# Moving the second pair's normalisation and the weight transposes within the first feed-forward stage of a gated multi-layer kernel

## What is computed

```python
def act_quant(x):                      # per token
    scale = 128.0 / clip(max(abs(x)), 1e-5)
    return clip(round(x * scale), -128, 127) / scale

gate = act_quant(x) @ ternary(w_gate).T        # 256 -> 1024
up   = act_quant(x) @ ternary(w_up).T
h    = silu(gate) * up
y    = act_quant(fwht(h)) @ ternary(w_down).T  # 1024 -> 256, fwht: Walsh-Hadamard transform
x    = x + tanh(g_ffn[1]) * y
```

## Time and profile before

| | |
|---|---|
| median of 3 runs | 758.43 us (758.4 to 760.88) |
| the profiled execution | 758.4 us, its span 756.6 us |
| PE busy | 673.2 us (89%), 4446 matmuls |
| DVE busy | 537.9 us (71%) |
| ACT busy | 350.4 us (46%) |
| POOL busy | 217.3 us (29%) |

### The profile page before, as it was taken

How to read it: one execution, slowest core, us unless ns; L and a number is a source line. 1 busy time by engine, 2 the same in 40 slices (tenths; PEclk the granted TensorE clock), 3 DMA queues, 4 the chain that set the end, 5 groups by cost and what they waited for, 6 DMA issues and landing times. The chain is left out here.

```text
span 756.6 us, 13927 instructions
## 1 busy us (share of the span) xinstructions
PE 673.2 (89%) x4446; PEld 461.8 (61%) x4446; DVE 537.9 (71%) x1622; ACT 350.4 (46%) x620; POOL 217.3 (29%) x308
## 2 busy tenths in 40 slices
PE   8999979798987987899779999986788999999997
PEld 4644566775864665587667787553243327777776
DVE  5687988877988788878866563747986957425545
ACT  2673545565464765142116325335488794122220
POOL 1001596101100033111314552632343220523330
PEclk9999996998999999989999999997799999999999
DMA  6997521050000050000063160012000043233214
GB/s 182 342 248 136 166 85 55 4 169 0 3 3 1 9 161 1 1 0 1 29 197 111 52 216 22 29 37 78 2 3 2 3 154 78 71 102 109 93 56 173
DMA packets 55565, 60.23 MB, mean 80 GB/s; under 512 B 13847, under 2 KB 48808, under 8 KB 55496
## 3 DMA queue, kind: packets, MB, share of 16 engines
q1 hardware_dynamic: 50408, 46.02, 21.4%
q0 software_dynamic: 4848, 13.28, 5.0%
q10 hardware_dynamic: 240, 0.05, 0.0%
HBM read 34.92 MB, written 24.20 MB: 78 GB/s over the span
## 5 line engine op out<-in xcount | busy, mean ns | idle before, releaser
L2040 ACT ACTIVATE arenas<-psum 128x512 f32<-128x512 f32 (+6 forms) x89 | 63.1, 732 | 52.6 <-PE psum L1188 46.2
L3342 DVE TENSOR_REDUCE arenas<-psum 128x2 f32<-128x512 f32 x96 | 61.8, 684 | 12.6 <-PE psum L1791 11.2
L996 POOL TENSOR_SCALAR arenas<-arenas,small 128x1024 f32<-128x1024 f32 x8 | 9.0, 1127 | 147.6 <-DVE small L3029 147.6
L1188 PE MATMUL psum<-conb,shared 128*128 128x128 bf16 (+2 forms) x512 | 39.2, 234 | 12.1 <-POOL shared L1001 5.1
L1013 POOL DMA_INDIRECT experts_l<-shared,small x30 | 29.7, 991 | 65.2 <-ACT shared L2348 54.9
L1188 PEld LDWEIGHTS psum<-conb,shared 128*128 128x128 bf16 (+2 forms) x512 | 34.7, 121 | 20.4 <-issue 12.8
L2040 ACT ACTIVATE late<-psum 128x512 f32<-128x512 f32 (+1 forms) x51 | 25.7, 504 | 40.8 <-PE psum L1188 40.8
L1188 PE MATMUL psum<-con,early 128*128 128x128 f32 (+1 forms) x188 | 32.5, 283 | 10.7 <-DVE early L2721 2.9
L2395 ACT ACTIVATE early<-psum 128x1024 f32<-128x1024 f32 x32 | 32.0, 1031 | 17.6 <-PE psum L1808 17.3
L1675 PE MATMUL psum<-early,late 128*128 128x256 f32 x128 | 33.4, 411 | 5.3 <-DVE early L3235 5.2
L1675 PE MATMUL psum<-arenas,early 128*128 128x256 f32 x160 | 36.7, 383 | 0.7 <-DVE arenas L3496 0.7
(11 more groups left out here) (455 smaller groups left out, 1780.4 us busy)
## 6 DMA issues: line engine op xcount, KB each, us to landing
sorted_l<-late SPq DMA_DIRECT2D x3, 1920.0 KB, 18.0
early<-sorted_l SPq DMA_DIRECT2D x6, 645.0 KB, 5.8
early<-in_L_ffn_sw SPq DMA_DIRECT2D x3, 1024.0 KB, 9.0
late<-sorted_l SPq DMA_DIRECT2D x23, 129.0 KB, 2.1
sorted_l<-late SPq DMA_DIRECT2D x1, 2944.0 KB, 23.7
early<-in_L_ffn_We_gate_up SPq DMA_DIRECT2D x2, 1408.0 KB
early<-in_L_ffn_expert_w SPq DMA_DIRECT2D x2, 1024.0 KB, 6.7
early<-in_L_ffn_w SPq DMA_DIRECT2D x1, 2048.0 KB, 8.4
```

The source lines that it names most:

```text
L996: pool.tensor_scalar(ha[s][:, rows], ha[s][:, rows], c2[s][:, t:t + 1], ROUND, ALU.mult, ALU.add)
L1188: last = pe.transpose(v[0:parts, at:at + k], src, idn[0:k, 0:k])
L2040: act.activation(dst, view(v), ACT.Copy, scale=scale).then_inc(f.drained(i, key), 1)
L3342: dve.tensor_reduce(nm, q3d(f.slot(0, ("max", w, k)), 2, S), X, ALU.max, negate=True)\
```

## The change

```diff
-        beside_f1 = [6, 7, 8, 9, 10, 11, 15, 16, 17, 18, 22, 23, 24, 25, 26, 27, 31, 32, 33, 34, 35, 36, 40, 41, 44]
+        beside_f1 = paced(6, (22, 1.5)) + [41, 45, 48]
...
                 second = second_rows()
-                advance(second, 1)
                 yield from steps(2)
...
-                            if step == 0:
-                                advance(second, 2)
-                            elif step == 1:
-                                advance(second, 1 + h)
+                            next(second, None)
                             yield
```

## The result

| | before | after |
|---|---|---|
| median of 11 runs each | 759.31 us (754.24 to 760.98) | 764.20 us (762.55 to 767.57) |
| the profiled execution, its span | 758.4 us, 756.6 us | 758.5 us, 756.7 us |

The changed kernel is slower: ratio 1.0065, 95% interval 1.004 to 1.009, or 4.9 us. The forecast was +3.1 us, 761.5; the time lies at the upper edge of the range, and the chance of 0.64 had gone to "no difference".

What follows compares the result with a forecast made beforehand. The stage from 239 to 321 us was taken as bound by a loop over DVE, POOL and PE, then by DVE; delays and savings up to transform(3) summed to +3.1 us, 758.4 to 761.5, range 757.9 to 764.2.

Steps and rivals of the forecast that it cites:

- One fill fewer ahead of had(0): Between tile 2's products and hT(1), one fill less on PE makes had(0) and transform(0) 0.5 us earlier.
- The late parts: Maxima and quantisation of the second pair, 3.99 us on DVE, now ahead of transform(1), which begins 3.5 us later.
- From yT(0) to had(2): PE's stretch with two fills instead of four: 4.8 us instead of 5.55, had(2) at 276.4.
- The fills in a row behind had(2): P14, P15 and P16 ahead of yT(1) without other work, paced 1.35 us apart by bank 0; yT(1) at 281.5.
- The early parts: Statistics, root and norm parts of second_rows on DVE, up to had(0): moving them costs nothing.
- P15 and P16: Two fills on PE between had(2) and yT(1); they account for 1.4 us of the forecast loss.
- +1.7 for free fills: The total loss in us if P15 and P16 cost nothing and yT(1) went at 280.1.
- transform(1) begins at 265.1 + 1.46 + 3.99: On DVE, transform(1) starts at 270.55 instead of 267.07, behind tile 3's product halves and the late parts.
- The port meeting: DVE and POOL lengthening each other on their shared port, weighed at transform(1); either way the sum stays +3.1 us.
- The clock rival: PE's clock falls ahead of dn(0), +2.4 us on top, 763.9; chance 0.32 together with other causes above +3.8.
- P23 and P24 in the wait ahead of yT(3): Two fills moved into PE's wait: no cost; they would keep the clock up, saving dn(1) 1.7 us, time unchanged.
- dn(1) short: Sign that the prediction is right: dn(1) on PE, 3.60 us before against 1.92 for dn(0), becomes short.

Runs made afterwards that it cites:

- b2: The changed kernel without POOL's clip of tile 0, so that POOL's pass of that tile ends sooner; ratio to the kernel before 1.0006.
- a1: The kernel before with only the move of second_rows on DVE, the table of fills as before; ratio to the kernel before 1.0026.
- e3: The changed kernel with unread matmuls in PE's waits, those of e2 and of b1; ratio to the kernel before 1.0042.
- a4: The changed kernel with two fills, P15 and P16, behind yT(1) and dn(0) instead of ahead of yT(1); ratio to the kernel before 1.004.
- d4: The changed kernel with twelve unread matmuls ahead of qT(1), no POOL clip of tile 0, and P15 and P16 behind yT(1); ratio to the kernel before 1.0003.
- a2: The kernel before with only the new table of fills, second_rows on DVE as before; ratio to the kernel before 1.0018.
- b1: The changed kernel with twelve unread 128x512 matmuls on PE in its waits ahead of qT of the second pair; ratio to the kernel before 1.0018.
- c1: The kernel before, DVE order untouched, with another table: fewer fills ahead of had(2) and had(3), the last in the wait ahead of yT(3); ratio 0.9981.
- a3: The kernel before with only the last two parts of second_rows (maxima, quantisation) moved behind tile 3's product halves; ratio to the kernel before 1.0034.
- e1: The kernel before with unread matmuls on PE about qT(0), ahead of yT(3) and ahead of dn(1); ratio to the kernel before 0.9956.
- e2: The run e1 with eight more unread matmuls ahead of yT(0); ratio to the kernel before 0.994.

## Why the prediction was right in direction and too small

By its own steps, each from the first maxima or the transform before (forecast, after, b2):

| step | forecast | after | b2 |
|---|---|---|---|
| to transform(0) | 20.65 | 20.48 | 20.47 |
| transform(0) to (1) | 11.05 | 12.03 | 11.17 |
| (1) to (2) | 7.95 | 9.17 | 7.82 |
| (2) to (3) | 12.70 | 12.57 | 12.57 |
| sum, over before's 49.30 | +3.05 | +4.95 | +2.73 |

**Right.** One fill fewer ahead of had(0), -0.5: -0.65. The late parts at 3.99 us between the product halves and transform(1): 4.08 in b2 (11.17 - 7.09). From yT(0) to had(2) 4.8 us: 4.71 in b2 (272.82 to 277.53). The fills in a row behind had(2), 1.35 apart: 280.21, 281.50, 282.85. DVE carries the delay to 321 in full. No fill waited for a transfer.

**Right in the number, not in the reason.** The early parts at nothing: the argument was that PE, up to had(0), waits for ACT and not for DVE. a1 and e3 show PE waiting 1.05 us for DVE there; slow first products covered it in the changed kernel. And P15 and P16 at 1.4 us: a4 gives 1.5, but with the clock fallen ahead of it; at full clock, as the prediction had it, they cost 0.3 (b2 to d4), so the +1.7 for free fills was too low. Behind it stands a transform(1) put at 5.63 us up to its L3029. It took 5.98, with a pause of 0.42 us ahead of L3025 that this tile had before as well (0.43 at 272.37), so POOL and yT(1) are later than forecast even without fills. In the fills' new place behind yT(1) they cost 0.46 more (yT(1) to transform(3) takes 10.18 us in d4 and 9.72 in b2).

**The step that failed, first: "transform(1) begins at 265.1 + 1.46 + 3.99".** The port meeting was weighed only for transform(1). POOL's pass of tile 0 starts when transform(0) has come to its L3029, and the late parts stand right behind that, so they are what meets it. The order of events was in the numbers of the prediction: POOL until 269.0, the late parts from 266 to 270. What the row shows is a wait until POOL ends, 1.02 instead of 0.17 us, and b2 shows the cause. By the Trainium skill (SBUF — State Buffer, Terms) the port pair that the two share is held for the full instruction and the loser blocks; the trace agrees, 268.83 and 268.85. The mistake was to take the size of the instruction for the size of the price: a step on 128x4 numbers pays as much as a large one. The trace of the kernel before already had such a case, which the prediction overlooked. Its DVE and its POOL:

```profile
295.86 0.93 DVE L2495 SCALAR_TENSOR_TENSOR small<-small 128x4 f32<-128x4 f32 x1
```

```profile
295.62 1.16 POOL L996 TENSOR_SCALAR arenas<-arenas,small 128x1024 f32<-128x1024 f32 x1 [8.31 <-DVE small L3029]
```

The step, 0.16 us elsewhere in the trace, ends at 296.79 and POOL's at 296.78.

**Second: "I take 4.8: had(2) 276.4" took a full clock for granted.** The clock rival was there with 763.9 us, but for dn(0), where the clock stayed at 1.00. It fell one stretch earlier, behind qT, and cost 1.35 us instead of 2.4. The prediction had named that stretch as sparse, but put no price on it. That the rival's time lies so near 764.2 is not a hit. The argument against it, 1.40 of 3.90 us busy with the clock at 1.00, is what misled: after had 1.49 of 3.90 and fell. One trace in which a gap did no harm says little about the next.

**Third: P23 and P24 in the wait ahead of yT(3).** "dn(1) short" was wrong in the profile of the changed kernel, and right in all others with fills there. PE in order of time: yT(3) before; yT(3) and dn(1) after; dn(1) in a2:

```profile
299.23 1.03 PE L1188 MATMUL psum<-conb,shared 128*128 128x128 bf16 x8 [3.09 <-POOL shared L1001]
```

```profile
304.10 0.62 PE L1188 MATMUL psum<-conb,shared 128*128 128x128 bf16 x8 [0.55 <-POOL shared L1001]
305.84 3.29 PE L1658 MATMUL psum<-early,arenas 128*128 128x256 bf16 x16 [1.12 <-ACT arenas L2040]
```

```profile
303.19 1.92 PE L1658 MATMUL psum<-early,arenas 128*128 128x256 bf16 x16 [1.12 <-ACT arenas L2040]
```

The wait for POOL shrank from 3.09 to 0.55 us, and dn(1) still took 3.29 us, mostly at the low clock. But a2, a4, b1, b2, c1 and d4 have fills in this wait too, PE waits 0.56 us or less there, and dn(1) took 1.92 us in each. With the wait left open (3.09, 3.05 and 3.06 us in before, a1 and a3) it took 3.60, 3.22 and 3.24, and with twelve wide matmuls in it (e1 to e3) 1.91. The Trainium skill (TensorE: Matmul & The Clock Gate, Why this matters for your kernels) asks for no long idle gap between bursts; twelve of the thirteen kernels agree with it here, after doesn't. It cost nothing in the sum, as forecast, since DVE is the limit there.

**The chances.** The sum of +3.1 lay under the 3.8 us that one can tell from no change, and 0.64 followed. What was left out of the sum (the meeting, the clock) could only add to it, so more of the chance belonged above +3.8.

**What stays open.** The stages of the profiles and the ratios agree in order, but not in size: in most kernels the ratio times 765 gives 1 to 3 us less than the stage's difference to before (b2 +2.7 and +0.5, e2 -1.7 and -4.6). So that both are 4.9 in the changed kernel is in part chance. Part of that can be the clock behind 321, which was low in the profile of before (and of e3, 6.35 us for the sixteen); that the other runs of before lose as much in places of their own is likely from their spread (754.24 to 760.98), and not shown.

## What to carry to other kernels

When work is moved on an engine, put every moved instruction, the small ones too, against what the engines it shares a port with run at that moment, not only the large step named in the argument. A wait of PE can cost twice, since the clock can fall behind it, but only if nothing else holds the path meanwhile, as POOL did in a1, a3 and a4. So prices found one by one need not add up. Matmuls into a bank that is free anyway, sized to fit the wait, gave 0.6% here without touching the order. And moving work out of a long wait (2.67 us ahead of transform(0), which the late parts had shortened at no cost) to make the pace even is a loss from the start: even is not the same as hidden.

## What the runs showed of the hardware

- A 128x4 step on DVE, 0.17 us by itself, takes 1.02 to 1.04 us when POOL's pass over 128x1024 is under way; it ends 0.01 to 0.03 us behind POOL's instruction. Seen in six kernels (after, a1, a3, a4, b1, e3), gone when the pass ended first (b2, d4). Another, L2495, took 0.86 to 0.93 us beside POOL's L996 in all thirteen.
- The same wait of PE, 2.03 us ahead of yT(0), was followed by a clock of 1.00 in before and by 0.58 over 270 to 272 in e1, whose code up to there differs only in nine matmuls about qT(0), some 25 us earlier. After, a1, a3, a4 and c1 all fell between 268 and 277; before, a2, b1, b2, d4, e2 and e3 did not.
- dn(1) of 1.92 us took 3.22 to 3.60 in the three kernels in which PE stood idle for some 3.1 us ahead of yT(3), and 1.91 or 1.92 in nine of the ten in which fills or other matmuls stood in that wait.
